# Turning both halves of a batch's heads in one visit instead of two

## The reference

```python
qh = einsum('bnd,hde->bhne', layernorm(x), Wq)
kh, vh = einsum('bmd,hde->bhme', ctx, Wk), einsum('bmd,hde->bhme', ctx, Wv)
att = softmax(einsum('bhne,bhme->bhnm', qh, kh) * 0.125, axis=-1)
out_h = einsum('bhnm,bhme->bhne', att, vh)          # 16 heads of 8 numbers for each row
concat = out_h.transpose(0, 2, 1, 3).reshape(B, N, 128)
x = x + tanh(g_xattn) * einsum('bnd,od->bno', concat, Wo)
# then: layernorm, router, top 2 of 8 experts, two matmuls with gelu in each expert,
# weighted and added back: x = x + tanh(g_ffn) * moe(layernorm(x))
```

## Time and profile before

| | us |
|---|---|
| median of 3 runs | 1299.17 |
| the 3 runs | 1294.05, 1299.71, 1299.17 |
| the profiled execution | 1296.63 |
| its span, first to last instruction | 1294.8 |

### The profile page before, as it was taken

The page is one execution under the profiler, slowest core; times in us unless marked ns, Lnnn a source line. Parts: engine busy times, 40 slices in busy tenths (PEclk is TensorE's granted clock), DMA queues, the critical chain, the costliest instruction groups (busy, mean ns, idle before and its releaser), DMA issues.

```text
span 1294.8 us, 42224 instructions
## 1 busy us (share of the span) xinstructions
PE 1248.2 (96%) x16259; PEld 629.0 (49%) x16259; DVE 1123.0 (87%) x2012; ACT 1085.2 (84%) x2196; POOL 553.5 (43%) x1213
## 2 busy tenths in 40 slices
PE   7999999999999999999999999999999999999992
PEld 2344444444444444444444444444444444499992
DVE  7889999999999999999999999999999999356434
ACT  2788998999898989999999998999999898866661
POOL 6324344353536262726252635445353512146551
PEclk9999999999999999999999999999999999999996
DMA  3332222212121212131212121222211110388896
GB/s 95 90 91 65 66 78 60 68 55 73 50 77 47 79 48 80 43 87 37 82 42 71 54 69 60 65 66 60 69 55 42 51 43 6 98 254 245 264 272 229
DMA packets 61092, 112.94 MB, mean 87 GB/s; under 512 B 13052, under 2 KB 36476, under 8 KB 60748
## 3 DMA queue, kind: packets, MB, share of 16 engines
q1 hardware_dynamic: 54187, 97.98, 25.8%
q0 software_dynamic: 4320, 8.99, 2.0%
q10 hardware_dynamic: 2385, 3.27, 0.7%
HBM read 52.77 MB, written 13.71 MB: 51 GB/s over the span
## 4 chain that ended last, share of the span: by engine, by line
PE 75%; SPq 9%; POOL 7%; DMA 3%; issue 2%; DVE 2%; ACT 1%; ACTq 0%; POOLq 0%; DVEq 0%
PE pv L912 28%; PE st L821 16%; PE mxp L875 12%; SPq L416 7%; PE st L798 6%; PE st L1130 5%; PE mxp L1140 5%; POOL kf L659 2%; DVE mx L1679 2%; POOL ksp L664 2%; POOL rows L723 1%; POOL ksp L662 1%; DMA qpack<-mxT 1%; POOL ksp L656 1%; DMA arena<-results 1%
## 5 line engine op out<-in xcount | busy, mean ns | idle before, releaser
L1679 DVE TENSOR_REDUCE mx<-mxp 128x2 f32<-128x1024 f32 x768 | 916.3, 1217 | 42.6 <-PE mxp L875 35.2
L1169 ACT ACTIVATE arena<-st 128x512 f32<-128x512 f32 (+1 forms) x1664 | 883.8, 597 | 66.8 <-PE st L821 53.1
L912 PE MATMUL pv<-arena 128*32 128x256 f32 x6656 | 531.6, 391 | 0.6 <-ACT pv_sb L1176 0.3
L821 PE MATMUL st<-qpack,kpack 51*128 51x256 bf16 (+1 forms) x3328 | 486.2, 272 | 4.9 <-DMA qpack<-mxT 4.6
L875 PE MATMUL mxp<-kpack,qpack 48*128 48x512 bf16 x1502 | 406.3, 382 | 1.3 <-DVE mx L1679 1.3
L821 PEld LDWEIGHTS st<-qpack,kpack 51*128 51x128 bf16 (+1 forms) x3328 | 195.1, 95 | 279.0 <-ACT arena L1169 149.6
L912 PEld LDWEIGHTS pv<-arena 128*32 128x32 f32 x6656 | 131.2, 108 | 173.8 <-issue 104.4
L690 POOL CAST mxs<-nmx 128x8 bf16<-128x8 f32 x64 | 12.2, 191 | 344.9 <-DVE nmx L1689 344.7
L875 PEld LDWEIGHTS mxp<-kpack,qpack 48*128 48x128 bf16 x1502 | 123.0, 93 | 67.2 <-issue 38.8
L1332 ACT ACTIVATE arena<-st,bias 128x256 f32<-128x256 f32 (+1 forms) x172 | 74.9, 437 | 45.5 <-PE st L1130 42.0
L723 POOL DMA_INDIRECT rows<-xrow,pos x64 | 65.9, 1030 | 89.9 <-DVE pos L1534 75.1
(11 more groups left out here) (202 smaller groups left out, 990.1 us busy)
## 6 DMA issues: line engine op xcount, KB each, us to landing
kpack<-ksp SPq DMA_DIRECT2D x756, 50.0 KB
arena<-in_w12T SPq DMA_DIRECT2D x43, 576.0 KB, 4.8
arena<-in_ctxT SPq DMA_DIRECT2D x15, 800.5 KB, 4.6
qpack<-qsp SPq DMA_DIRECT2D x187, 32.0 KB
xblk<-rows SPq DMA_DIRECT2D x28, 132.0 KB, 4.2
rows<-in_pads SPq DMA_DIRECT2D x8, 264.0 KB
arena<-results SPq DMA_DIRECT2D x8, 256.0 KB, 6.8
arena<-results ACTq DMA_DIRECT2D x8, 256.0 KB, 7.4
```

The lines of the kernel that those rows point to most:

```text
L821: ins = eng.matmul(ring[i][0:n, jj * N:(jj + 1) * N], kpack[rows, b % 2, g * JJ + jj, kt * P:kt * P + n], qpack[rows, b % 2, g * JJ + jj, ...
L912: ins = eng.matmul(pv[32 * j:32 * j + 32, 0:N], vaug[0:n, b % 2, kt, at:at + 32], pt[0:n, (2 * u + rg) % PT_BUFS, jj * N:(jj + 1) * N], st ...
L1169: eng.activation(pt[0:n, c % PT_BUFS, :], ring[bank_of["S", u, p]][0:n, :], ACT.Exp, scale=SCALE).then_inc(s_exp, 1)
L1679: eng.tensor_reduce(mx[:, tj, w, :], src[:, :, 0:WIN], AX.X, ALU.max).then_inc(s_red, 1)
```

## The change

`HEADS_AT` becomes the single number 3. At r = 3 of batch b+1 PE turns both halves of batch b, with four transposes into all 512 columns of one bank, and DVE makes one reciprocal of 32 denominators per row and one product of 256 numbers. The visit at r = 47 is gone, and with it one bank taken from the ring per batch. ACT's copy into `pv_sb` waits for the turn of a whole batch before. `conc` is laid out by halves, and the rows of `woT` are ordered to match on the host. After the last batch both halves are turned in the one visit at q = 2.

```diff
--- before.py
+++ after.py
@@ -97,7 +97,7 @@
 PHASES = [(0, FULL, SL), (FULL, LARGE - FULL, SL), (LARGE, NBK - LARGE, SS)]
 K_AT = {1: 0, 4: 1, 5: 2, 8: 3}
 V_AT = {25: 0, 26: 1, 27: 2, 30: 3}
-HEADS_AT = {3: 0, 47: 1}
+HEADS_AT = 3
 TURN_AT, PLACE_AT = {8: 1, 22: 2, 31: 3, 47: 4}, {9: 1, 23: 2, 31: 3, 49: 4}
 POST_AT = {7: "C", 9: "F", 21: "L", 23: "R"}
 X_AT, Q_AT = 36, 42
@@ -177,8 +177,8 @@
         take("S", u, 1)
         if r in TURN_AT and b * NG + TURN_AT[r] < GROUPS:
             take("M", b * NG + TURN_AT[r])
-        if r in HEADS_AT and b * TWOS + HEADS_AT[r] > 0:
-            take("H", b * TWOS + HEADS_AT[r] - 1)
+        if r == HEADS_AT and b > 0:
+            take("H", b - 1)
         if prepared(b, r):
             take(*prepared(b, r))
         if b == 0 and r in FIRST_V_AT:
@@ -191,8 +191,7 @@
             take("N", b - 1)
         if b == B - 1 and r == COUNT_AT:
             take("T", 0)
-    at["H", COPIES - 1] = ST_BUFS
-    for kind in (*POST_AT.values(), "N"):
+    for kind in ("H", *POST_AT.values(), "N"):
         at[kind, B - 1] = ST_BUFS
     at["T", 1] = ST_BUFS
     return at
@@ -276,9 +275,9 @@
         xn = sb("xn", [P, NT, D])
         xnT = sb("xnT", [P, N])
         pv_sb = sb("pv_sb", [P, 2, N])
-        conc = sb("conc", [P, NT, HG, NG, DH])
+        conc = sb("conc", [P, NT, TWOS, HG, 2, DH])
         concT = sb("concT", [P, N])
-        rden = sb("rden", [P, NT * HG, 2])
+        rden = sb("rden", [P, TWOS * NT * HG, 2])
         mx = sb("mx", [P, NT * JJ, NW, RG])
         nmx = sb("nmx", [P, NT * HG])
         mxr = sb("mxr", [P, NT * HG])
@@ -982,23 +981,24 @@
                         ins.then_inc(s_vp, 1)
                 freed[i] = s_v, NV * b + c + 1
 
-            def turn_heads(k):
-                i = bank_of["H", k]
+            def turn_heads(b):
+                i = bank_of["H", b]
                 eng.wait_ge(*freed[i])
-                eng.wait_ge(s_pvs, k + 1)
-                for t in range(NT):
-                    ins = eng.transpose(ring[i][:, t * P:(t + 1) * P],
-                                        pv_sb[:, k % 2, t * P:(t + 1) * P], id_sb[:, :])
+                eng.wait_ge(s_pvs, TWOS * (b + 1))
+                for k in range(TWOS):
+                    for t in range(NT):
+                        ins = eng.transpose(ring[i][:, (t * TWOS + k) * P:(t * TWOS + k + 1) * P],
+                                            pv_sb[:, k, t * P:(t + 1) * P], id_sb[:, :])
                 ins.then_inc(s_f1p, 1)
-                freed[i] = s_conc, k + 1
+                freed[i] = s_conc, b + 1
 
             def turn_concat(b):
                 i = bank_of["C", b]
                 eng.wait_ge(*freed[i])
-                eng.wait_ge(s_conc, TWOS * (b + 1))
+                eng.wait_ge(s_conc, b + 1)
                 for t in range(NT):
                     ins = eng.transpose(ring[i][:, t * P:(t + 1) * P],
-                                        conc[:, t, :, :, :].rearrange("p j g e -> p (j g e)"),
+                                        conc[:, t, :, :, :, :].rearrange("p k j g e -> p (k j g e)"),
                                         id_sb[:, :])
                 ins.then_inc(s_f2p, 1)
                 freed[i] = s_concT, b + 1
@@ -1072,8 +1072,8 @@
                     weighted(u - LAG)
                 if r in TURN_AT and b * NG + TURN_AT[r] < GROUPS:
                     turn_maxima(b * NG + TURN_AT[r])
-                if r in HEADS_AT and b * TWOS + HEADS_AT[r] > 0:
-                    turn_heads(b * TWOS + HEADS_AT[r] - 1)
+                if r == HEADS_AT and b > 0:
+                    turn_heads(b - 1)
                 if b + 1 < B:
                     if r in keys_at(b):
                         keys(b + 1, keys_at(b)[r])
@@ -1145,7 +1145,7 @@
                 if c == 2 and i + 1 < NBK:
                     turn_in(i + 1)
                 if q == 2:
-                    turn_heads(COPIES - 1)
+                    turn_heads(B - 1)
                 elif q == 6:
                     turn_concat(B - 1)
                 elif q == 9:
@@ -1171,8 +1171,8 @@
 
             def copy_weighted(k):
                 eng.wait_ge(s_pv, 2 * KT * (k + 1))
-                if k > 1:
-                    eng.wait_ge(s_f1p, k - 1)
+                if k >= TWOS:
+                    eng.wait_ge(s_f1p, k // TWOS)
                 eng.activation(pv_sb[:, k % 2, :], pv[:, 0:N], ACT.Copy).then_inc(s_pvs, 1)
 
             def copy_rows(b):
@@ -1702,21 +1702,20 @@
                     eng.tensor_scalar(qearly[:, h, :], q_first[:, 0:N], head_rows[:, h:h + 1], None,
                                       ALU.mult).then_inc(s_qearly, 1)
 
-            def divide(k):
+            def divide(b):
 
                 nonlocal own
-                b, two = divmod(k, TWOS)
-                eng.wait_ge(s_f1p, k + 1)
-                fin = ring[bank_of["H", k]][:, 0:N].rearrange("p (q c) -> p q c", c=32)[:, :, 0:VP]
+                eng.wait_ge(s_f1p, b + 1)
+                fin = ring[bank_of["H", b]][:, 0:TWOS * N].rearrange("p (q c) -> p q c", c=32)[:, :, 0:VP]
                 fin = fin.rearrange("p q (g c) -> p q g c", c=VC)
                 eng.reciprocal(rden[:, :, :], fin[:, :, :, DH]).then_inc(s_dve, 1)
                 own += 1
                 eng.wait_ge(s_dve, own)
-                if two == 0 and b > 0:
+                if b > 0:
                     eng.wait_ge(s_f2p, b)
                 eng.tensor_tensor(
-                    conc[:, :, :, 2 * two:2 * two + 2, :].rearrange("p t j g e -> p (t j) g e"),
-                    fin[:, :, :, 0:DH], rden[:, :, :].unsqueeze(3).to_broadcast([P, NT * HG, 2, DH]),
+                    conc[:, :, :, :, :, :].rearrange("p t k j g e -> p (t k j) g e"),
+                    fin[:, :, :, 0:DH], rden[:, :, :].unsqueeze(3).to_broadcast([P, TWOS * NT * HG, 2, DH]),
                     ALU.mult).then_inc(s_conc, 1)
 
             def add_attention(b):
@@ -1755,8 +1754,8 @@
                 for w in windows(u, 0):
                     maximum(*w)
                 small(b, r, 0)
-                if r in HEADS_AT and b * TWOS + HEADS_AT[r] > 0:
-                    divide(b * TWOS + HEADS_AT[r] - 1)
+                if r == HEADS_AT and b > 0:
+                    divide(b - 1)
                 if b > 0 and r in POST_AT:
                     if POST_AT[r] == "F":
                         add_attention(b - 1)
@@ -1829,7 +1828,7 @@
                 if c == 3 and 0 <= i - 1 < NBK:
                     add_bias(i - 1)
                 if q == 3:
-                    divide(COPIES - 1)
+                    divide(B - 1)
                 elif q == 10:
                     add_attention(B - 1)
                 elif 11 <= q < 14:
@@ -1892,7 +1891,7 @@
         "wq": halves(a["L0_xattn_Wq"]),
         "wk": groups(a["L0_xattn_Wk"]),
         "wv": heads(a["L0_xattn_Wv"]),
-        "woT": a["L0_xattn_Wo"].T.reshape(NG, HG, DH, D).transpose(1, 0, 2, 3).reshape(D, D),
+        "woT": a["L0_xattn_Wo"].T.reshape(TWOS, 2, HG, DH, D).transpose(0, 2, 1, 3, 4).reshape(D, D),
         "rwT": a["L0_ffn_router_w"].T,
         "w12T": np.concatenate([
             a["L0_ffn_w1"].transpose(2, 0, 1),
```

## The result

| | before | changed |
|---|---|---|
| median of 11 runs, us (lowest to highest) | 1298.82 (1294.05 to 1301.88) | 1292.52 (1290.77 to 1294.79) |
| ratio, 95% interval | | 0.9959 (0.9946 to 0.9972) |
| profiled execution, its span | 1296.63, 1294.8 | 1290.77, 1289.0 |

The changed kernel is 0.41% faster. The changed kernel itself was measured on the first chip and on those two; on the other two, which take as long as the first, only variants of it ran.

The account below looks back on a forecast made before the run. PE was taken to bound the batch loop, DVE 3.2 us behind. Terms 0 + 0.38 + 2.6 - 1.75 = +1.2 us on a base of 1297.9 gave 1299.1 us, range 1293.5 to 1304.

Parts of the forecast that it names:

- the 15 visits at r = 3 cost 15 x 0.38: nothing in sum: PE's transposes: 15 x 0.37 given back at r = 47, 15 x 0.38 paid at r = 3, sum 0.
- The new wait, +2.6: r = 3 to 5: PE waits for DVE's longer hold, 0.17 us a batch beyond its own work, fifteen times.
- the estimate from the eight repeated steps: Reciprocal at r = 3: 16 more elements cost 133 ns where the rows give 102, the pair 0.80 instead of 0.77.
- The gain at r = 47: Dropping two transposes at r = 47 saves PE 0.37 us in batches 0 to 14, nothing in batch 15.
- What the queue gives back: Ahead of r = 26: arriving 0.55 later shortens five batches' waits for the maxima's transfer, -1.75 us.
- The experts' transposes: At q = 2 of the experts' loop, batch 15's two transposes moved from r = 47 add 0.38 us.
- Number 2: Rival: DVE is the bound and its saving of 0.31 us in each of 15 batches shows; 1293.6 us, chance 0.08.
- Rival 1: The bank costs nothing at r = 4, PE only 0.38 late at r = 26; 1296.8 us, chance 0.20.
- Rivals 3 and 4: 3: longer hold at r = 3 paid fully, 1304.5, chance 0.09; 4: dropping r = 47 gains nothing, 1304, 0.05.
- Rival 3: Pair at r = 3 above about 0.7 us delays r = 5; doubled, 0.56 a batch, 1304.5 us, chance 0.09.

Follow-up runs that it names:

- Numbers 3: Kernel before with both halves' visits at r = 3, in two banks with two divisions: 1296.76 against 1298.78 us, ratio 0.9984.
- number 5: Kernel before with each visit of the heads making its two transposes twice: 1303.87 against 1297.84 us, ratio 1.0046.
- number 6: Changed kernel with r = 3's four transposes ahead of the weighted sum: 1308.12 us against 1310.23 of the kernel before, ratio 0.9989.
- number 4: Changed kernel with its one division cut in two pairs of reciprocal and product: 1299.6 us against 1298.78 of the kernel before, ratio 1.001.

## Why the prediction was wrong

**The step that failed is "the 15 visits at r = 3 cost 15 x 0.38: nothing in sum".** It took the price of two transposes as the same wherever they stand. Two more in a visit that is there cost 0.21, so the term was 15 x 0.21 = 3.2 and not 5.7: 2.5 us mis-sized. The trace of before hinted at it. PEld loads the weights of the two transposes in 0.20 us, where the visit holds PE for 0.37:

```profile
311.10 0.20 PEld L990 LDWEIGHTS st<-id_sb,pv_sb 128*128 128x128 f32 x2
```

In the changed kernel four loads take 0.42, so each further one 0.11, and the further pair costs just that, 0.21, while a visit alone pays some 0.16 beside its two. Numbers 3 and 5 show it without the rest of the change. The Trainium skill, page "TensorE: Matmul & The Clock Gate", section "LDWEIGHTS (loading the stationary operand)", gives a load of P columns P/1.2 ns, 107 for 128. The trace is near it: the third and fourth load each add 0.11, and number 5 gives 0.216 for two. But the profile's record of a single one of these loads is 0.14 us long, and no run separates whether the loads or the transposes themselves set the step. What the fixed 0.16 consists of (the first load, uncovered, would be most of it) no run took apart; number 6 shows only that it doesn't depend on what stands ahead.

**The new wait, +2.6, was too large: +0.54.** Its parts came as told: the reciprocal took 0.36, the product 0.42 (forecast 0.35 and 0.42), the key chunk's weights waited, the window of r = 5 was 0.10 later. But with the row of transposes 0.17 shorter than assumed, DVE idled 0.23 and not 0.4 ahead of the reciprocal, and the next maximum came 0.41 later rather than 0.62 (counted from the unit's start), so the bank at r = 4 cost nothing. Of the 1.61 at r = 5, 1.07 was given back at r = 8, where DVE's lag had been a wait already. The bounds of this term, 0 and 0.56 a batch, held it. The prices under it were right. The product took 425 ns, where the formula of the Trainium skill, page "VectorE: DVE Perf Modes", section "The TRN2 errata — SBUF-src ops pay a fixed extra latency per instruction", gives 424; the page states it for an addition. The reciprocal took 358 ns, the 356 of the rows and not the 387 of the estimate from the eight repeated steps.

**The gain at r = 47** came, 0.37 in 16 batches and not 15: in the last batch I took it for lost because PE waits for a transfer afterwards, but that transfer was itself earlier, and PE started the experts 5.4 earlier.

**What the queue gives back**, -1.75, was -2.23, of which 0.50 is batch 0, where nothing stands at r = 3. The other -1.73 hits the forecast by luck. PE comes to r = 25 only 0.19 us later in a batch, not 0.55. On the other hand r = 25 is longer than its plain 2.00 in eight of these batches of the kernel before (by 0.08 to 1.07) and not in five, and two of them shrank by more than 0.19 (0.35 and 0.49), which is not explained. **The experts' transposes**, +0.38, were +0.22. **Not foreseen**: r = 16, -0.72. Terms against measurement: 0, +2.6, -1.75, +0.38 against -2.67, +0.54, -2.23, +0.22, so +1.2 against -4.1. The rest of the 5.9 us between the two profiled executions is r = 16, r = 9 of batch 0 and some 0.9 behind the last unit's start, less the 0.3 ahead of the first.

**Rivals.** Number 2 named the nearest time (1293.6) for the wrong reason: DVE is busy 0.34 less in the stretch, but PE is busy for all of it, and the gain stands at r = 47 and r = 3, where PE's own transposes take less. Rival 1 (no cost at r = 4) is what happened at that place, and gave 1296.8, since it kept the mis-sized term. Rivals 3 and 4 fell: r = 5 grew by 0.10 and not by 0.56, and r = 47 gained its 0.37 in every trace of the changed kernel. Rival 3 was right in that there is such a point: with two pairs in number 4 the hold cost 0.26 a batch, at r = 4 and not at r = 5.

**On chips C and D next to nothing is left.** The intervals reach from 0.998 to 1.001, so a gain of 2 us is not excluded, and the traces of chip D leave 1.7 us in the units. The greater part of the gain is eaten, not by anything that the forecast had, but by results around r = 5 that come late when an indirect DMA stands some 0.6 us ahead of it; the change moved the one against the other (the DMA starts 0.37 ahead of r = 5 in the kernel before, 0.59 in the changed one).

## What to carry to other kernels

Price a step by what it adds to a run of like instructions, not by its mean: a further transpose cost 0.108, a visit of two 0.37. Behind a change that shifts one engine's steps by tenths, look at which instructions of the others now start together, since that decided more than 3 us twice here. And repeat a gain of half a per cent on another chip: 0.9959 on one was 0.9998 on another.
